# Alternating sums and weighing as a loop of 16 pairs, with all products on DVE

## The chip, the core and the metric

The kernel runs on one core of a Trainium2 chip. The metric is the time of one execution on the device in microseconds (us). A core has TensorE (PE), VectorE (DVE), ScalarE (ACT), GpSimd (POOL) and SyncE (SP), which run their own instruction streams and meet at semaphores. TensorE multiplies a stationary operand, which a weight load brings in, with a moving one, and writes to PSUM.

## What is computed

The reference is a compressed interaction network of two layers, for 512 samples with 39 fields of 64 values each, in float32:

```python
x0 = x                                  # (512, 39, 64)
h1 = einsum('bid,bjd,ijh->bhd', x0, x0, W0)   # W0 (39, 39, 128)
h2 = einsum('bid,bjd,ijh->bhd', x0, h1, W1)   # W1 (39, 128, 128)
out = concatenate([h1, h2], axis=1).sum(axis=-1)   # (512, 256)
```

Since the last sum is over d, both halves of the output are weighted sums of values that don't depend on the weights: sums over d of products of two fields (first half) or three fields (second half) of one sample.

## The kernel before

Setup. TensorE multiplies W1 with the symmetric part of W0 (L568), ACT copies the result out of PSUM (L513), DVE and GpSimd add up its entries to one weight for every product of three fields (L338, L232), TensorE turns these by transposes (L576) and ACT copies them into place (L517, 27 copies). They are 105 lists of 128 x 128 weights at c0; 10 more lists for products of two fields are loaded at c1_0.

Then the samples. Two samples are a pair: the 64 values d of each are half of the 128 partitions. 64 pairs (128 samples) are a batch, 8 pairs a unit, so there are 4 batches and 32 units. For a unit:

- SP loads x_w (windows of fields, the stationary operands of the sums; L307, two places) and x_d (fields in the order in which DVE needs them; L315, three places, DS).
- The products of two fields, 4 columns of 115 slots per pair, are written to one of two places (PRODS): DVE makes most (L422, L425, semaphore prod_ready), GpSimd five small ones (L286, L290, rest_ready), and ACT copies 10 slots of single fields (L531, singles_ready).
- TensorE sums over d (L591, `sum_four`): 12 matmuls per pair of 64 rows by 32 columns, 96 per unit, into two PSUM banks per four pairs. ACT copies the banks to s0 (L542), where a slot then has 128 columns, one for each sample of the batch.
- When a batch is summed, its 115 slots are weighed (L611, `weigh`): the slot is the stationary operand of a 128 x 128 x 128 matmul, its list the moving one, and all add up in one of two output banks. ACT copies this out (L524) and sends it to memory.

A matmul of float32 shows as two MATMUL and two LDWEIGHTS records in the trace.

TensorE's order is written out by hand. The 8 units of the first batch run as a loop of two units with 4 turns. Units 8 to 31 are unrolled: behind the sums of each unit stand 14 or 15 slots of the batch before. The last batch's 115 slots come at the end. The sums of a unit wait for all three makers of its products, and each four for the banks; products of a unit wait until the sums of the unit two before are through, since they write to the same place. SP issues in its own order, and waits for each load's place to be free.

Of the kernel before, what the change touches and what calls it, by code (L numbers as in the profile page):

```python
# [23 lines left out]
FIELDS = 39  # L24
# [77 lines left out]
def cin_kernel(nc: bass.Bass, x_w: bass.AP, x_d: bass.AP, w0: bass.AP, w1: bass.AP, c1: bass.AP, out: bass.AP):  # L102
# [12 lines left out]
    PRODS, WS, DS = 2, 2, 3  # L115
    WORDS = 56064
# [3 lines left out]
    with ctx:  # L120
# [21 lines left out]
        d_0 = take(DS * UNIT * D_WORDS)  # L142
        out_sb0 = take(2 * HID)
# [12 lines left out]
        assert w0_second0 + Y_WIDTH <= d_0 and c1_second0 + SINGLES * HID <= out_sb0  # L156

        banks = [ctx.enter_context(nc.psum_tensor(f"stage{i}", [P, BANK], F32)) for i in range(6)]
        out_ps = [ctx.enter_context(nc.psum_tensor(f"out_ps{i}", [P, BANK], F32)) for i in range(2)]
# [18 lines left out]
        rest_ready = sem("rest_ready")  # L178
        singles_ready = sem("singles_ready")
        batch_done = sem("batch_done")  # L180
        out_copied = sem("out_copied")
# [37 lines left out]
        def _(pool):  # L219
# [56 lines left out]
            for u in range(UNITS):  # L276
                pool.wait_ge(d_loaded[u % DS], 16 * (u // DS + 1))
                if u < PRODS:
                    pool.wait_ge(z_ready, 1)
                else:  # L280
                    pool.wait_ge(filled, filled_through_unit(u - PRODS))
                d, to = d_0 + u % DS * UNIT * D_WORDS, prod0 + u % PRODS * UNIT * PROD
                for column, slot, w, x in TRIANGLES:
                    n, x_at = len(block(x)), d + D_AT[x]
                    if n % 2 == 0:
                        nc.gpsimd.tensor_tensor(view(to + column * LISTED + slot + n * n // 2, (PROD, UNIT), (1, n // 2)),  # L286
                                                view(x_at, (D_WORDS, UNIT), (1, n // 2)),
                                                view(x_at + n // 2, (D_WORDS, UNIT), (1, n // 2)), ALU.mult)
                for column, slot, w, b0, b1 in LONE_LISTS:
                    done = nc.gpsimd.tensor_tensor(view(to + column * LISTED + slot, (PROD, UNIT), (1, b1 - b0)),  # L290
                                                   view(d + D_B + b0, (D_WORDS, UNIT), (1, b1 - b0)),
                                                   view(d + D_LONE, (D_WORDS, UNIT), (0, b1 - b0)), ALU.mult)
                done.then_inc(rest_ready, 1)

        @block_.sync
        def _(sp):
# [13 lines left out]
            def load_listed(u):  # L310
                if u >= DS:
                    sp.wait_ge(prod_ready, u - DS + 1)
                    sp.wait_ge(rest_ready, u - DS + 1)
# [12 lines left out]

            for u in range(WS, UNITS):
                if u + 1 < UNITS and u + 1 >= DS:
                    load_listed(u + 1)
                load_windows(u)  # L330

        @block_.vector
        def _(dve):
# [78 lines left out]
            def products(u):  # L412
# [6 lines left out]
                for column, slot, w, x in TRIANGLES:  # L419
# [3 lines left out]
                         view(x_at, D, (1, whole), (1, n)), ALU.mult)  # L423
                for column, slot, w, x, x0, x1, y, g0, g1 in RECTANGLES:
# [83 lines left out]
        def _(act):  # L508
            g = 0
            for f in range(FIELDS):  # L510
                for a, b in Y_PARTS:
                    act.wait_ge(filled, g + 1)
                    nc.scalar.copy(view(y0 + f * Y_WIDTH + a, (1, b - a)), banks[g % RING][:, 0:b - a]).then_inc(emptied, 1)  # L513
                    g += 1
            for k, n in TURNS:
                act.wait_ge(filled, g + 1)
                nc.scalar.copy(view(c0 + k * HID, (1, n * HID)), banks[g % RING][:, 0:n * HID]).then_inc(emptied, 1)  # L517
                g += 1

            def take_out(n):  # L520
                act.wait_ge(batch_done, n + 1)
                if n >= 1:
                    act.wait_ge(out_stored, 16 * n)
                nc.scalar.copy(view(out_sb0, (1, 2 * HID)), out_ps[n % 2][:, 0:2 * HID]).then_inc(out_copied, 1)  # L524
                act.wait_ge(out_copied, n + 1)
                act.dma_start(out[n * B:(n + 1) * B, :], view(out_sb0, (1, 2 * HID))).then_inc(out_stored, 16)

# [6 lines left out]

            act.wait_ge(z_ready, 1)
            for u in range(PRODS):
                singles(u)
            for q in range(FOURS):
                n, t = divmod(q * FOUR, PAIRS)
                act.wait_ge(filled, SETUP_BANKS + q + 1)  # L540
# [4 lines left out]
                u = (q + 1) * FOUR // UNIT - 1  # L545
# [3 lines left out]
                if t == PAIRS - FOUR and n >= 1:  # L549
                    take_out(n - 1)  # L550
# [4 lines left out]
        def _(pe):  # L555
# [43 lines left out]
            def weigh(n, k):  # L599

                if k == 0:
                    pe.wait_ge(emptied, emptied_through_four((n + 1) * PAIRS // FOUR - 1))
                    if n == 0:
                        pe.wait_ge(c1_ready, 1)
                    if n >= 2:
                        pe.wait_ge(out_copied, n - 1)
# [88 lines left out]
```

## Time and profile before

| | us |
|---|---|
| median of 3 runs | 345.33 (340.78 to 349.36) |
| the profiled execution | 343.26 |
| its span, first to last instruction | 341.5 |
| PE busy in it | 263.6 (77%) |
| DVE busy | 200.4 (59%) |
| ACT busy | 129.1 (38%) |
| POOL busy | 114.8 (34%) |

The profile is of one execution. Busy shares are averages over stages that differ: the setup lasts until 96.75 us, the first batch until about 140, then sums and weighing alternate until 309.65, and the last batch is weighed. "issue" stands where an engine was idle and waited for nothing that the profile shows. PE's busy time counts overlapping matmuls once.

### The profile page before, as it was taken

Reading aid. Unit: us, or ns where it says so; the run is one execution under the profiler, and the core shown is the slowest. Engines: PE = TensorE matmul, PEld = TensorE weight load, DVE = VectorE, ACT = ScalarE, POOL = GpSimd, SP = SyncE. Lnnn points to the kernel's source line nnn. Section 1 sums busy time; section 2 is a strip of 40 time slices with the busy share of each in tenths; the row PEclk is TensorE's granted clock in tenths of the full one; section 3 lists DMA queues with packets and bytes.
Section 4 is the critical chain, followed back from the end, with each engine's and each line's share of the span. In section 5 each row is a group of like instructions: output and inputs, shape, how many; then the busy total and the mean of one; then the engine's idle time right before and its main releaser. Section 6 shows DMA issues by size and latency. Waiting matters only on the chain.

```text
span 341.5 us, 16183 instructions
## 1 busy us (share of the span) xinstructions
PE 263.6 (77%) x7325; PEld 226.8 (66%) x7325; DVE 200.4 (59%) x671; ACT 129.1 (38%) x270; POOL 114.8 (34%) x284
## 2 busy tenths in 40 slices
PE   0999999206946516848988788899798878889997
PEld 0555555106935515738878778788788778779996
DVE  1125599999436977935567675686577766730000
ACT  1477777203954415511333234323343224322000
POOL 9425596304022694662233222332232222300000
PEclk9999999755996968876999999999999999999999
DMA  7800000400034625622334443353335433200000
GB/s 263 370 0 0 5 0 0 161 1 0 2 111 136 184 68 189 195 56 101 101 101 145 114 142 118 105 192 103 102 112 168 131 105 103 73 23 19 0 2 15
DMA packets 10860, 32.56 MB, mean 95 GB/s; under 512 B 1200, under 2 KB 1712, under 8 KB 10672
## 3 DMA queue, kind: packets, MB, share of 16 engines
q1 hardware_dynamic: 10224, 31.15, 28.4%
q8 instruction: 48, 0.79, 0.9%
q10 hardware_dynamic: 576, 0.52, 0.4%
q14 instruction: 12, 0.10, 0.1%
HBM read 31.14 MB, written 0.52 MB: 93 GB/s over the span
## 4 chain that ended last, share of the span: by engine, by line
PE 70%; issue 17%; DVE 5%; ACT 4%; DMA 2%; POOL 2%; SPq 0%; DVEq 0%; POOLq 0%
PE out_ps L611 31%; PE stage L591 22%; PE stage L568 16%; DVE arena L425 3%; ACT arena L517 3%; DVE arena L422 2%; DMA arena<-in_w 2%; PE stage L576 2%; POOL arena L286 1%; ACT arena L542 0%; ACT arena L531 0%; POOL arena L290 0%; SPq L298 0%; SPq L297 0%; ACT arena L524 0%
## 5 line engine op out<-in xcount | busy, mean ns | idle before, releaser
L591 PE MATMUL stage<-arena 64*32 64x115 f32 (+4 forms) x6144 | 87.0, 244 | 45.2 <-issue 32.6
L611 PE MATMUL out_ps<-arena 128*128 128x128 f32 x920 | 111.3, 280 | 4.4 <-issue 4.4
L542 ACT COPY arena<-stage 128x460 f32<-128x460 f32 x128 | 63.1, 545 | 132.9 <-PE stage L591 131.4
L611 PEld LDWEIGHTS out_ps<-arena 128*128 128x128 f32 x920 | 106.5, 194 | 9.1 <-issue 8.6
L591 PEld LDWEIGHTS stage<-arena 64*32 64x32 f32 x6144 | 75.5, 110 | 53.7 <-issue 51.0
L286 POOL TENSOR_TENSOR arena<-arena 128x24 f32<-128x24 f32 x96 | 52.8, 575 | 158.7 <-PE stage L591 144.1
L422 DVE TENSOR_TENSOR arena<-arena 128x224 f32<-128x224 f32 (+1 forms) x192 | 62.1, 389 | 71.2 <-PE stage L591 71.1
L425 DVE TENSOR_TENSOR arena<-arena 128x392 f32<-128x392 f32 (+5 forms) x288 | 91.4, 386 | 0.0
L568 PE MATMUL stage<-arena 128*128 128x390 f32 x156 | 54.3, 511 | 7.7 <-DMA arena<-in_w 7.7
L338 DVE TENSOR_TENSOR arena<-arena 128x294 f32<-128x294 f32 (+30 forms) x189 | 47.5, 327 | 15.1 <-ACT arena L513 15.0
L568 PEld LDWEIGHTS stage<-arena 128*128 128x128 f32 x156 | 30.8, 198 | 30.5 <-issue 10.4
L513 ACT COPY arena<-stage 128x390 f32<-128x390 f32 x78 | 37.7, 484 | 22.7 <-PE stage L568 22.7
L232 POOL COPY arena<-arena 128x6 f32<-128x6 f32 (+21 forms) x117 | 28.4, 303 | 24.4 <-ACT arena L513 24.4
L576 PE MATMUL stage<-arena 128*128 128x128 f32 x105 | 14.1, 306 | 18.1 <-issue 18.1
L576 PEld LDWEIGHTS stage<-arena 128*128 128x128 f32 x105 | 13.9, 161 | 18.7 <-issue 18.7
L290 POOL TENSOR_TENSOR arena<-arena 128x88 f32<-128x88 f32 x64 | 23.0, 379 | 0.0
L517 ACT COPY arena<-stage 128x512 f32<-128x512 f32 (+1 forms) x27 | 13.5, 682 | 20.0 <-PE stage L576 20.0
L531 ACT COPY arena<-arena 128x320 f32<-128x320 f32 x32 | 15.8, 505 | 0.0
L524 ACT COPY arena<-out_ps 128x256 f32<-128x256 f32 x4 | 1.5, 372 | 33.9 <-PE out_ps L611 33.9
L220 POOL MEMSET arena<- 128x13440 f32 x1 | 11.3, 11298 | 0.3 <-POOLq L684 0.3
L435 DVE TENSOR_TENSOR arena<-arena 128x1280 f32<-128x1280 f32 x1 | 1.5, 1492 | 9.9 <-DMA arena<-in_c 9.9
L432 DVE TENSOR_TENSOR arena<-arena 128x780 f32<-128x780 f32 x1 | 1.0, 971 | 5.0 <-DMA arena<-in_w 5.0
(7 smaller groups left out, 2.2 us busy)
## 6 DMA issues: line engine op xcount, KB each, us to landing
arena<-in_x_d SPq DMA_DIRECT2D x32, 448.0 KB, 4.0
arena<-in_x_w SPq DMA_DIRECT2D x32, 360.0 KB, 3.3
arena<-in_w SPq DMA_DIRECT2D x1, 1344.0 KB, 10.1
arena<-in_c SPq DMA_DIRECT2D x2, 640.0 KB, 11.7
arena<-in_w SPq DMA_DIRECT2D x2, 390.0 KB, 3.4
arena<-in_w SPq DMA_DIRECT2D x1, 768.0 KB, 7.4
out<-arena ACTq DMA_DIRECT2D x4, 128.0 KB, 1.7
arena<-in_w SPq DMA_DIRECT2D x1, 384.0 KB, 5.9
```

The source lines that it names most:

```text
L232: return nc.gpsimd.tensor_copy(view(to, *to_axes), view(at, *axes))
L286: nc.gpsimd.tensor_tensor(view(to + column * LISTED + slot + n * n // 2, (PROD, UNIT), (1, n // 2)), view(x_at, (D_WORDS, UNIT), (1, n // 2)),
L338: return nc.vector.tensor_tensor(view(to, *to_axes), view(a, *a_axes), view(b, *b_axes), ALU.add)
L422: mult(view(at, T, (n, whole), (1, n)), view(x_at, D, (0, whole), (1, n)), view(x_at, D, (1, whole), (1, n)), ALU.mult)
L425: done = mult(view(to + column * LISTED + slot, T, (g1 - g0, x1 - x0), (1, g1 - g0)), view(d + D_AT[x] + x0, D, (1, x1 - x0), (0, g1 - g0) ...
L513: nc.scalar.copy(view(y0 + f * Y_WIDTH + a, (1, b - a)), banks[g % RING][:, 0:b - a]).then_inc(emptied, 1)
L517: nc.scalar.copy(view(c0 + k * HID, (1, n * HID)), banks[g % RING][:, 0:n * HID]).then_inc(emptied, 1)
L542: nc.scalar.copy(view(s0[n % 2] + s * PAIRS + t, (B, LISTED), (1, FOUR)), banks[2 * (q % 2) + s][:, 0:LISTED * FOUR].rearrange("p (n b) -> ...
L568: nc.tensor.matmul(claim(g)[:, 0:b - a], view(w1_0 + f * HID, (1, HID)), view(w0_0 + a, (1, b - a)), start=True, stop=True).then_inc(fille ...
L576: done = nc.tensor.transpose(bank[:, m * HID:(m + 1) * HID], view(z0 + (k + m) * B, (1, B)), view(ident0, (1, HID)))
L591: done = nc.tensor.matmul(banks[2 * four_place + s][WIDE * column:WIDE * (column + 1), 0:LISTED * FOUR] .rearrange("p (n b) -> p b n", b=F ...
L611: done = nc.tensor.matmul(to, view(s0[n % 2] + k * B, (1, B)), weights, start=k == 0, stop=k == LISTED - 1, skip_group_check=True)
```

## The change

- Units 8 to 31 are no longer unrolled on TensorE but a loop over three batches with a loop of 4 turns inside, each of two units: 16 pairs. Its instructions are the same in each turn, so the slots to weigh must lie at a fixed place: ACT copies 13 slots a unit of the batch before to t_0, in a half of 6 and one of 7, and TensorE weighs them from there. The list (moving operand) is found by an address in a register. The 11 slots left (all 10 singles and one) are copied and weighed behind each batch's last unit. The last batch is weighed unrolled and from s0, as before.
- There is one output bank instead of two. A matmul with zeros (GpSimd clears the identity for that) begins it for both halves.
- DVE makes the five small products as well, 20 instructions a unit instead of 15; GpSimd makes none, and rest_ready is gone.
- x_d has two places instead of three (the room goes to t_0), and SP issues each unit's x_d just ahead of its x_w, one unit later than before.
- ACT copies the singles of the first two units ahead of the turned lists instead of behind them.

TensorE, where unit 8 ends and its first weighing stands; stage are the banks of sums, out_ps the output's. Before:

```order
L591 MATMUL stage<-arena 32x57 x2
L591 MATMUL stage<-arena 32x115 x4
L611 MATMUL out_ps<-arena 128x128 [waits c1_ready,emptied]
L611 MATMUL out_ps<-arena 128x128 x13
L591 MATMUL stage<-arena 32x49 [waits singles_ready,rest_ready,emptied,prod_ready,w_loaded1]
```

And now, in the inner loop (ISA is a fused instruction of two to four register operations):

```order
L614 MATMUL stage<-arena 32x57 x2
L614 MATMUL stage<-arena 32x115 x4
L678 ISA [waits staged]
L630 MATMUL out_ps<-arena 128x128
L630 ISA
L630 MATMUL out_ps<-arena 128x128
L630 ISA
L630 MATMUL out_ps<-arena 128x128
L630 ISA
L630 MATMUL out_ps<-arena 128x128
```

A register instruction now stands between each two slots, and a wait for ACT's copy ahead of each half.

ACT in a unit of the later batches; L542 and L557 empty the banks of sums, L531 and L509 copy the singles. Before:

```order
L542 COPY arena<-stage 128x115x4 [waits filled]
L542 COPY arena<-stage 128x115x4
L542 COPY arena<-stage 128x115x4 [waits filled]
L542 COPY arena<-stage 128x115x4
L531 COPY arena<-arena 128x32x10 [waits d_loaded0]
```

And now:

```order
L541 COPY arena<-arena 128x768 [waits weighed]
L541 COPY arena<-arena 128x896 [waits weighed]
L557 COPY arena<-stage 128x115x4 [waits filled]
L557 COPY arena<-stage 128x115x4
L557 COPY arena<-stage 128x115x4 [waits filled]
L557 COPY arena<-stage 128x115x4
L509 COPY arena<-arena 128x32x10 [waits d_loaded0]
```

Two copies of 6 and 7 slots stand ahead of the banks, and wait for TensorE's weighing of the half before in the same place.

The diff, cut to what is spoken of:

```diff
-    PRODS, WS, DS = 2, 2, 3
+    PRODS, WS, DS = 2, 2, 2
+
+    IN_BATCH = PAIRS // UNIT
+    EACH = PAIRED // IN_BATCH
+    HALVES = [(0, EACH // 2), (EACH // 2, EACH)]
+    REST = LISTED - IN_BATCH * EACH
+    REST_HALVES = [(0, EACH // 2), (EACH // 2, REST)]
...
-            for u in range(UNITS):
-                pool.wait_ge(d_loaded[u % DS], 16 * (u // DS + 1))
...
+            pool.wait_ge(filled, SETUP_BANKS)
+            nc.gpsimd.memset(ident, 0.0).then_inc(out_free, 1)
...
-            for u in range(WS, UNITS):
-                if u + 1 < UNITS and u + 1 >= DS:
-                    load_listed(u + 1)
+            for u in range(DS, UNITS):
+                load_listed(u)
                 load_windows(u)
...
+                    if n % 2 == 0:
+                        mult(view(at + n * n // 2, T, (1, n // 2)), view(x_at, D, (1, n // 2)),
+                             view(x_at + n // 2, D, (1, n // 2)), ALU.mult)
+                for column, slot, w, b0, b1 in LONE_LISTS:
+                    mult(view(to + column * LISTED + slot, T, (1, b1 - b0)), view(d + D_B + b0, D, (1, b1 - b0)),
+                         view(d + D_LONE, D, (0, b1 - b0)), ALU.mult)
...
+            def stage(first, a, b, half):
+                if half >= 2:
+                    act.wait_ge(weighed, half - 1)
+                nc.scalar.copy(view(t_0 + a * B, (1, (b - a) * B)), view(first + a * B, (1, (b - a) * B)))\
+                    .then_inc(staged, 1)
...
+                if n >= 1 and t % UNIT == 0:
+                    for i, (a, b) in enumerate(HALVES):
+                        half = (n - 1) * IN_ALL + v * len(HALVES) + i
+                        stage(s0[(n - 1) % 2] + (SINGLES + v * EACH) * B, a, b, half)
...
+            def begin_out():
+                nothing = view(ident0, (1, HID))
+                nc.tensor.matmul(out_ps[:, 0:2 * HID], nothing, view(ident0, (0, 2), (1, HID)), start=True, stop=False,
+                                 skip_group_check=True)
...
+            def weigh_staged(v, a, b):
+                for k in range(a, b):
+                    done = weigh(t_0 + k * B, c0 + k * HID + v * (EACH * HID), False)
+                done.then_inc(weighed, 1)
...
+            def turn(w_wanted, unit_wanted, banks_wanted, behind):
+                for v in range(PRODS):
+                    pe.wait_ge(w_loaded[v], w_wanted)
+                    pe.wait_ge(prod_ready, unit_wanted)
+                    pe.wait_ge(singles_ready, unit_wanted)
+                    pe.reg_add(unit_wanted, unit_wanted, 1)
+                    for half in range(2):
+                        pe.wait_ge(emptied, banks_wanted)
+                        pe.reg_add(banks_wanted, banks_wanted, 2)
+                        sum_four(v, half, half)
+                    behind(v)
+                pe.reg_add(w_wanted, w_wanted, 16)
...
+                with pe.Fori(1, BATCHES):
+                    pe.wait_ge(out_free, out_wanted)
+                    pe.reg_add(out_wanted, out_wanted, 1)
+                    begin_out()
+                    with pe.Fori(0, IN_BATCH, PRODS) as first:
+                        def weigh_unit(v):
+                            for a, b in HALVES:
+                                staged_half()
+                                weigh_staged(first + v, a, b)
+                        turn(w_wanted, unit_wanted, banks_wanted, weigh_unit)
+                    for a, b in REST_HALVES:
+                        staged_half()
+                        weigh_rest(t_0, t_0 + SINGLES * B, a, b).then_inc(weighed, 1)
```

## Rows read from the trace of the kernel before

**Rows 1.** Stages; columns: stretch, length, PE, PEld, DVE, ACT, POOL busy, clock, DMA.
```profile
96.75:139.96 43.21, 23.37 (x1536) 20.77 (x1537) 32.39 (x106) 18.13 (x39) 21.73 (x36) 0.80 0.49 146
139.96:161.68 21.72, 15.06 (x448) 13.75 (x452) 13.28 (x45) 5.36 (x12) 12.50 (x15) 0.76 0.38 117
161.68:309.65 147.97, 127.45 (x4829) 118.40 (x4829) 95.35 (x300) 50.66 (x108) 36.42 (x100) 1.00 0.36 112
```

**Rows 2.** Groups of PE, 161.68 to 309.65; columns: form, count, busy, mean ns, idle before.
```profile
L611 PE MATMUL out_ps<-arena 128*128 128x128 f32 x605 | 73.5, 279 | 3.5 <-issue 3.5
L591 PE MATMUL stage<-arena 64*32 64x115 f32 (+4 forms) x4224 | 57.2, 233 | 17.0 <-issue 17.0
```

**Rows 3.** The chain of waits, 176 to 185 us; columns: start, length, what.
```profile
175.99 2.39 PE stage L591 x116
178.38 3.32 PE out_ps L611 x28
...
183.25 0.91 issue
```

**Rows 4.** The timeline of PE, first batch and unit 9; columns: start, length, group, idle before.
```profile
106.16 1.23 PE L591 MATMUL stage<-arena 64*32 64x49 f32 x47 [2.16 <-issue]
...
107.56 2.73 PEld L591 LDWEIGHTS stage<-arena 64*32 64x32 f32 x192 [0.59 <-issue]
107.59 2.95 PE L591 MATMUL stage<-arena 64*32 64x49 f32 x192 [0.20 <-issue]
...
112.93 2.45 PE L591 MATMUL stage<-arena 64*32 64x49 f32 x192 [2.39 <-issue]
...
127.04 3.25 PE L591 MATMUL stage<-arena 64*32 64x49 f32 x192 [7.35 <-POOL arena L290]
...
149.72 2.11 PE L591 MATMUL stage<-arena 64*32 64x49 f32 x114 [2.86 <-issue]
```

**Rows 5.** The timeline of DVE and POOL in the first batch.
```profile
107.49 2.02 DVE L422 TENSOR_TENSOR arena<-arena 128x224 f32<-128x224 f32 x6 [3.40 <-PE stage L591]
...
109.44 3.20 DVE L425 TENSOR_TENSOR arena<-arena 128x392 f32<-128x392 f32 x9
...
115.53 10.51 POOL L286 TENSOR_TENSOR arena<-arena 128x24 f32<-128x24 f32 x3 [3.20 <-PE stage L591]
...
116.88 1.64 DVE L422 TENSOR_TENSOR arena<-arena 128x224 f32<-128x224 f32 x6
...
118.44 2.82 DVE L425 TENSOR_TENSOR arena<-arena 128x392 f32<-128x392 f32 x9
...
121.18 1.64 DVE L422 TENSOR_TENSOR arena<-arena 128x224 f32<-128x224 f32 x6
...
139.36 9.59 POOL L286 TENSOR_TENSOR arena<-arena 128x24 f32<-128x24 f32 x3 [4.27 <-PE stage L591]
```

**Rows 6.** DMA queues; columns: queue, kind, packets, MB, share of 16 engines.
```profile
q8 instruction: 48, 0.79, 0.9%
```

**Rows 7.** Groups of ACT, each shape apart, whole span.
```profile
L542 ACT COPY arena<-stage 128x460 f32<-128x460 f32 x128 | 63.1, 545 | 132.9 <-PE stage L591 131.4
...
L531 ACT COPY arena<-arena 128x320 f32<-128x320 f32 x32 | 15.8, 505 | 0.0
```

**Rows 8.** The timeline where the setup ends.
```profile
93.51 2.44 ACT L517 COPY arena<-stage 128x512 f32<-128x512 f32 x5
...
95.57 1.10 ACT L531 COPY arena<-arena 128x320 f32<-128x320 f32 x2
...
96.75 2.95 PE L591 MATMUL stage<-arena 64*32 64x49 f32 x210 [2.55 <-ACT arena L531]
```

**Rows 9.** The loads of x_d: from issue to landing.
```profile
DMA to landing us min/median/max: 3.3/4.0/4.9
```

**Rows 10.** The end of the chain of waits; columns as in rows 3.
```profile
309.72 29.24 PE out_ps L611 x260
...
338.98 0.37 ACT arena L524
```

More of the change, by code:

```diff
@@ L142, in cin_kernel @@
         d_0 = take(DS * UNIT * D_WORDS)
+        t_0 = take(EACH * B)
         out_sb0 = take(2 * HID)
@@ L155, in cin_kernel @@
         c1_second0 = d_0 + Y_WIDTH
-        assert w0_second0 + Y_WIDTH <= d_0 and c1_second0 + SINGLES * HID <= out_sb0
+        assert REST <= EACH and w0_second0 + Y_WIDTH <= d_0 and c1_second0 + SINGLES * HID <= out_sb0
         banks = [ctx.enter_context(nc.psum_tensor(f"stage{i}", [P, BANK], F32)) for i in range(6)]
-        out_ps = [ctx.enter_context(nc.psum_tensor(f"out_ps{i}", [P, BANK], F32)) for i in range(2)]
+        out_ps = ctx.enter_context(nc.psum_tensor("out_ps", [P, BANK], F32))
         RING = len(banks)
@@ L508, in _, with singles @@
         def _(act):
+            def singles(u):
+                act.wait_ge(d_loaded[u % DS], 16 * (u // DS + 1))
+                nc.scalar.copy(view(prod0 + u % PRODS * UNIT * PROD, (PROD, UNIT), (LISTED, 4), (1, SINGLES)),
+                               view(d_0 + u % DS * UNIT * D_WORDS + D_SINGLES, (D_WORDS, UNIT), (SINGLES, 4), (1, SINGLES)))\
+                    .then_inc(singles_ready, 1)
             g = 0
@@ L514, in _ @@
                     g += 1
+            act.wait_ge(z_ready, 1)
+            for u in range(PRODS):
+                singles(u)
             for k, n in TURNS:
@@ L549, in _ @@
                 if t == PAIRS - FOUR and n >= 1:
+                    (a, b), (_, c) = REST_HALVES
+                    half, s_at = n * IN_ALL - len(REST_HALVES), s0[(n - 1) % 2]
+                    stage(s_at, a, b, half)
+                    act.wait_ge(weighed, half)
+                    nc.scalar.copy(view(t_0 + b * B, (1, (SINGLES - b) * B)), view(s_at + b * B, (1, (SINGLES - b) * B)))
+                    nc.scalar.copy(view(t_0 + SINGLES * B, (1, (c - SINGLES) * B)),
+                                   view(s_at + (SINGLES + IN_BATCH * EACH) * B, (1, (c - SINGLES) * B)))\
+                        .then_inc(staged, 1)
                     take_out(n - 1)
@@ new lines, in weigh_staged, with weigh_rest @@
+            def weigh_staged(v, a, b):
+                for k in range(a, b):
+                    done = weigh(t_0 + k * B, c0 + k * HID + v * (EACH * HID), False)
+                done.then_inc(weighed, 1)
+            def weigh_rest(s_at, last_at, a, b):
+                for k in range(a, b):
+                    if k < SINGLES:
+                        done = weigh(s_at + k * B, c1_0 + k * HID, True)
+                    else:
+                        done = weigh(last_at, c0 + (PAIRED - 1) * HID, False, stop=True)
+                return done
@@ L647, in _, with staged_half @@
-            for k in range(LISTED):
-                weigh(BATCHES - 1, k)
+                    turn(w_wanted, unit_wanted, banks_wanted, lambda v: None)
+                pe.wait_ge(c1_ready, 1)
+                def staged_half():
+                    pe.wait_ge(staged, staged_wanted)
+                    pe.reg_add(staged_wanted, staged_wanted, 1)
+                with pe.Fori(1, BATCHES):
[11 more added lines that the diff above has]
+                        weigh_rest(t_0, t_0 + SINGLES * B, a, b).then_inc(weighed, 1)
@@ L651 @@
+            s_at = s0[(BATCHES - 1) % 2]
+            pe.wait_ge(out_free, BATCHES)
+            begin_out()
+            pe.wait_ge(emptied, emptied_through_four(FOURS - 1))
+            for k in range(IN_BATCH * EACH):
+                weigh(s_at + (SINGLES + k) * B, c0 + k * HID, False)
+            weigh_rest(s_at, s_at + (LISTED - 1) * B, 0, REST).then_inc(weighed, 1)
 def kernel(r_x, L0_rec_W0, L0_rec_W1):
```

92 lines of the change are left out of this document (19 added, 73 removed).

## The prediction

> **What bounds the kernel now.** The profiled execution took 343.26 us, its span is 341.5; the 1.8 between them is kept. It lies 2.1 under the median of the runs, 345.33. I read the busy time by stage first, then the groups of the longest stage, then the chain of waits, then the timeline where they left a question.
>
> By stage [rows 1]: the reader is to see that TensorE is busy 127.45 of 147.97 us in the long stretch, but only 23.37 of 43.21 in the first batch and 15.06 of 21.72 behind it, and that no other engine comes near it in the long stretch (DVE 95.35). In that stretch the two kinds of matmul stand side by side [rows 2]: 4224 records are 22 units of 192, 605 are 302 slots at two records each, and TensorE is idle for 20.5 us with nothing named as the releaser ("issue").
>
> One unit without and one with such a gap [rows 3]: the sums of a unit last 2.39 us, 14 slots of weighing 3.32, so 0.237 a slot, and in the next unit 0.91 us of nothing lie inside the sums. What the gaps are the first batch tells [rows 4]. There the code is a loop of two units. In its first turn TensorE stops in the middle of sums for 2.16 us at 106.16; in later turns 192 records run through in one piece (2.45 us at 112.93), on the same engine with the same kind of work. And the instruction queue fetched 48 packets, 0.79 MB, 16.4 KB each [rows 6]. 7325 matmul records and as many weight loads were executed; less three repeats of 768 that is 12,346, or 257 a packet: each instruction was fetched once, the loop's too. So the gaps are fetches of new code, which a second turn of a loop does not need.
>
> DVE and GpSimd set the first batch [rows 5]. DVE makes the products of a unit in 4.30 us (116.88 to 121.18) when it works alone. A GpSimd multiplication that starts at 115.53 does not end until DVE pauses; TensorE waits 7.35 us for it, until 127.04 [rows 4]. It happens again at 139.36, and the sums of unit 9 start only at 149.72 [rows 4, 5].
>
> **The change, part by part.**
>
> *Start of unit 0.* The two copies of singles stood behind ACT's last copy of the turned lists (end 95.95); unit 0 started at 96.75, just behind them [rows 8]. They now stand ahead of the 27 copies, where ACT waited for the first transposes anyway. Unit 0 starts at 96.03: -0.7.
>
> *DVE takes the five small products.* 6 multiplications of 1104 elements take 1.56 us and 9 of 2040 take 2.74 [rows 5], start to start: 68 ns each plus 1.04 ns an element. Five more with 216 elements: 0.57 us, 4.87 us a unit. In the long stretch that hides: DVE starts when a unit's sums end and must be done one weighing, one set of sums and one weighing later (3.1 + 2.4 + 3.1 us). In the first batch it is the bound. The first turn is as before, with its fetches: the sums of unit 1 ended 0.20 before 107.59 [rows 4] and now end 0.7 earlier, at 106.7; products 3 end at 111.6, then one unit each 4.87: products 8 end at 136.0 and the sums of unit 8 begin at **136.1**. Before they began at 139.96, and the next unit lost ten more.
>
> *Two places instead of three for the lists.* A load is issued when the products two units earlier are made and has 4.87 us; the loads take 3.3 to 4.9, median 4.0 [rows 9]. I cost it at nothing; at its slowest, with signals and issue 0.4 more, it adds 0.4 a unit in five units, 2 us. SP also asks for the lists one unit later than before, still behind the same product.
>
> *Code of units 8 to 31 as a loop of 12 turns.* Goes: 20.5 us of gaps in 22 units [rows 2] and those of units 8 and 9. Comes: a first pass through some 900 new instructions, 3 us by the 0.9 to 2.2 us of such gaps [rows 3, 4]. Comes too: at each unit register arithmetic, waits and every second time a branch. In the first loop that cost TensorE 0.20 us, its weight loads 0.59 [rows 4]; I take **0.4** at each unit.
>
> *Weighing by register address.* 13 slots a unit instead of 14.4, and 11 behind each batch. Each slot now has a fused register instruction ahead of it and a moving operand whose address a register holds. No row shows that form. From below: it hides under the 0.237 us that the array needs for a slot (nothing). A gain is excluded, since the same two passes stream. From above: 0.59 us for the six steps at a turn is 0.1 a step; with the dispatcher's share in the 0.4 us before that perhaps 0.15. Three slow steps a slot (register instruction, two passes) make 0.30 to 0.45, that is 0.06 to 0.21 too much for 312 slots, 20 to 66 us. I take nothing, since steady dispatch should be nearer to the middle of a stream than to a turn's branch and four waits, and keep both ends.
> The Trainium skill ("TensorE: Matmul & The Clock Gate", Wait — 56ns, not 53.3ns?) gives about 62 ns for a matmul that its sequencer decodes in software. By that the two passes would take 0.12 us, under 0.237, and my sum would stand; no run here shows the figure.
>
> *ACT copies 13 slots a unit, in halves.* 768 and 896 elements; from 320 elements in 0.505 us [rows 7] at best 0.88 and 0.99 (at 0.85 ns an element, the slope from 256 elements in 0.37 us [rows 10] to 460 in 0.545), at worst, by proportion, 1.21 and 1.41. With four copies of 0.545 and one of 0.505, overlapping a little, ACT has 4.4 to 5.3 us in a unit of 5.9. A half is copied as soon as TensorE is through with its predecessor, one unit ahead of need, so it hides; if it did not, ACT's lateness would be added to each unit.
>
> *One output bank, cleared by a matmul.* At each of three later batches TensorE waits for the copy-out (0.37 us as in [rows 10], with signals 0.6) and clears 256 columns (0.4): 3 us in all. GpSimd has nothing left, hence no stuck multiplication.
>
> **The sum.** 136.1; 24 units of 2.39 + 13 x 0.237 = 5.47: 131.3; 33 slots behind batches: 7.8; 24 x 0.4: 9.6; outputs 3; first pass 3. That is 290.8. The last 115 slots at 0.225 (29.24 us for 130 [rows 10]): 25.9; from there to the end of the span 2.5. Span 319.2, time **321.0**: 22 under the profiled execution, 7% under the median. Two per cent, 7 us here, is about what a measurement of this kernel tells from no change.
>
> **The rivals.**
>
> *The dispatcher becomes the bound, mildly (0.20).* A slot takes 0.25 to 0.32 us and the 0.4 becomes 0.6: 321 + 4 to 26 + 5, or 330 to 352. For it: three slow steps against 0.237 leaves little. The profile would show equal gaps between weighing matmuls.
>
> *The same, strongly (0.11): slower than before.* The place is the weighing in units 8 to 31, the price (slot - 0.237) x 312, and it decides from 0.337 us a slot: 321 + 31 = 352, 2% over the median. At 0.45 the time is 387. For it: the turn's six steps already take 0.1 each; against: mid-unit register steps leave no mark in 2.45 us of sums.
>
> *Code is fetched again at each turn (0.06): slower.* A turn would fetch 3.6 blocks. Before, 4829 x 2 instructions were 37.7 blocks for 20.5 us: 0.54 each; 12 turns add 23. The branch back would wait for its block, 2.16 seen plus the 1.6 us that the block ahead lasts: 43 more. 321 + 23 + 43 - 3 = 384. Against: [rows 6], and the turn at 107.59 that cost 0.20. For: the body is 909 instructions, the first loop's 780.
> The Trainium skill ("Runtime: NRT & Kernel Launch", Instruction fetch mechanics) has this rule: a taken branch out of a two-page window forces a fetch. By that rule it is 384; the trace of the first loop speaks against it.
>
> *Everything turns but the feeders are late (0.08).* DVE keeps its slower pace, 2.02 + 3.20 us [rows 5] plus 0.57, in the first batch (+6), or loads add 2, or ACT adds 2 at a batch's start: 325 to 334.
>
> *More comes back (0.05).* Boundaries hide wholly and the first pass under DVE: 308 to 313. That leaves **0.50** for the forecast, 313 to 330.
>
> **Numbers.** Faster by over 2% (under 338.4): 0.50 + 0.08 + 0.05 and half of the mild rival, 0.72. Within 2%: its other half and a bit, 0.11. Slower: 0.17. The range takes in the forecast, late feeders and most of the mild rival: 312 to 345.
>
> **What will show it.** PE's instruction queue with some 11 packets instead of 48. Products of a unit in 4.87 us; unit 8 near 136. Weighing at 0.237 a slot in units 8 to 31, against 0.225 in the tail, shows the register address right or wrong; gaps at each second unit show the branch. Weight-load gaps inside sums in later turns would prove me wrong on fetching, ACT's L541 as a releaser on staging.

## The result, and where the time went

| | us | ratio to before, 95% interval |
|---|---|---|
| before, median of 4 runs | 346.7 (340.78 to 349.36) | |
| changed kernel, median of 4 runs | 310.63 (309.65 to 311.24) | 0.905 (0.894 to 0.916) |
| predicted | 321.0, range 312 to 345 | 0.93 |

It is 9.5% faster. The ratio is taken over the runs in the faster of two states that executions of these kernels show (of before, 340.78 and 345.33), so it is not the quotient of the medians. The cause forecast is the one that the trace shows, and the gain is larger than forecast: 310.63 lies 10.4 under the predicted time and 1.4 under the range. The profiled execution took 310.69 us, its span is 308.9, so 1.8 lie outside the span as before.

The span is 32.6 shorter. Read at four marks that both traces have:

| | before | after | difference |
|---|---|---|---|
| up to the sums of unit 0 | 96.75 | 95.25 | -1.5 |
| units 0 to 7, up to the sums of unit 8 | 43.21 | 39.44 | -3.8 |
| units 8 to 31, up to the last batch's weighing | 169.76 | 146.00 | -23.8 |
| weighing of the last batch, and the end | 31.8 | 28.2 | -3.6 |

Marks of before are in [rows 1, 8, 10]; those of after follow. First the stages of the changed kernel, with the columns of [rows 1]:

```profile
95.25:134.69 39.44, 24.46 (x1538) 21.44 (x1539) 34.58 (x142) 19.70 (x41) 0.00 (x0) 0.83 0.53 157
134.69:279.99 145.30, 140.83 (x5302) 132.55 (x5302) 113.81 (x460) 103.24 (x178) 0.00 (x0) 1.00 0.40 128
```

In the first batch DVE is busy 34.58 of 39.44: it is still the bound there, behind the fetches of the loop's first turn. In the long stretch TensorE is busy 140.83 of 145.30, so 4.5 us are left of what were 20.5 in 22 units [rows 2]. ACT has come from 50.66 us of the long stretch of before to 103.24 here, and still TensorE waits for it only at the end of a batch, for the copy-out (0.38 in the chain below). From the page, the instruction queue and the two groups of matmuls (columns as in [rows 2]):

```profile
q8 instruction: 10, 0.16, 0.2%
...
L630 PE MATMUL out_ps<-arena 128*128 (+1 forms) x920 | 109.5, 278 | 1.3 <-issue 1.3
...
L614 PE MATMUL stage<-arena 64*32 64x115 f32 (+4 forms) x6144 | 82.9, 243 | 19.2 <-issue 11.6
```

Ten packets instead of 48 [rows 6]: at 256 instructions each that is 2560, while the 7333 matmul records and as many weight loads that were executed are 57 times 256. So the loops were not fetched again at each turn. Slots with a register address ahead of them have the mean of before (278 ns against 279).

The chain of waits from the first pass of the new loop on:

```profile
134.69 2.44 PE stage L614 x109
137.14 1.09 PE out_ps L630 x8
138.23 1.34 issue
139.57 2.27 PE out_ps L630 x18
141.84 1.30 PE stage L614 x67
143.15 1.57 issue
144.72 1.28 PE stage L614 x47
146.00 3.10 PE out_ps L630 x26
149.09 2.38 PE stage L614 x117
...
176.51 2.38 PE stage L614 x115
178.90 5.57 PE out_ps L630 x48
...
184.49 0.38 ACT arena L532
184.87 0.12 issue
185.00 0.67 PE out_ps L625 x2
...
280.69 25.70 PE out_ps L630 x230
...
```

Three things are to be seen. The first pass has two holes, 1.34 and 1.57, and the pieces of work beside them last 0.5 longer than in later units (14.41 us up to 149.10 for two units that later take 2 x 5.48). From 146.00 on a unit is 3.10 + 2.38 = 5.48 us with nothing between them, neither at a unit nor, every second time, at the branch. And a batch costs a copy of 0.38, 0.12 and a clear of 0.67 between 5.57 of weighing (24 slots) and the next sums. Apart from the first pass and these three pauses, the long stretch is TensorE's own work, end to end. The outer loop, which spans the inner one and the slots behind it, comes back without a gap too.

In units 10 to 31, 147.97 us before [rows 1] and 131.66 now (149.03 to 280.69), the gaps took 20.5. The bare work of before was 22 x 2.39 + 302 x 0.237 = 124.2, its busy time 127.45. The other 3.3 lie in sums that a gap cuts in two: they last 2.54 to 2.75 us in the chain of before instead of 2.39, here 1.55 + 1.01:

```profile
181.70 1.55 PE stage L591 x76
183.25 0.91 issue
184.16 1.01 PE stage L591 x45
```

The granted clock of that stretch was 1.00 [rows 1], so it is not the clock that draws them out. What does, no run here shows.

### The profile page after: what moved, and what is told of

It is laid out like the page before. It is cut to its first block, busy times and chain, and to the rows that moved or that the text cites. A ratio compares the mean times of both kernels' runs of the same rounds, so it can differ in the third digit from the quotient of the medians.

```text
span 308.9 us, 16634 instructions
## 1 busy us (share of the span) xinstructions
PE 259.3 (84%) x7333; PEld 224.4 (73%) x7333; DVE 208.3 (67%) x831; ACT 176.7 (57%) x327; POOL 40.6 (13%) x125
## 4 chain that ended last, share of the span: by engine, by line
PE 77%; issue 10%; DVE 6%; ACT 5%; DMA 2%; SPq 0%; DVEq 0%
PE out_ps L630 35%; PE stage L614 22%; PE stage L591 17%; ACT arena L524 4%; DVE arena L422 3%; DVE arena L413 2%; DMA arena<-in_w 2%; PE stage L599 1%; PE out_ps L625 1%; ACT arena L557 1%; ACT arena L532 0%; DVE arena L419 0%; DVE arena L416 0%; SPq L292 0%; SPq L291 0%
## 5 line engine op out<-in xcount | busy, mean ns | idle before, releaser
L630 PE MATMUL out_ps<-arena 128*128 (+1 forms) x920 | 109.5, 278 | 1.3 <-issue 1.3
L630 PEld LDWEIGHTS out_ps<-arena 128*128 128x128 f32 x920 | 104.8, 192 | 5.8 <-issue 5.8
L614 PE MATMUL stage<-arena 64*32 64x115 f32 (+4 forms) x6144 | 82.9, 243 | 19.2 <-issue 11.6
L614 PEld LDWEIGHTS stage<-arena 64*32 64x32 f32 x6144 | 74.2, 110 | 25.5 <-issue 23.0
L422 DVE TENSOR_TENSOR arena<-arena 128x392 f32<-128x392 f32 (+5 forms) x288 | 90.4, 386 | 0.0
L557 ACT COPY arena<-stage 128x460 f32<-128x460 f32 x128 | 63.2, 545 | 31.4 <-PE stage L614 28.8
L413 DVE TENSOR_TENSOR arena<-arena 128x224 f32<-128x224 f32 (+1 forms) x192 | 58.2, 344 | 31.2 <-PE stage L614 31.2
L541 ACT COPY arena<-arena 128x768 f32<-128x768 f32 (+1 forms) x51 | 44.8, 883 | 22.8 <-PE out_ps L630 21.8
L509 ACT COPY arena<-arena 128x320 f32<-128x320 f32 x32 | 15.5, 488 | 18.9 <-DVE arena L329 17.5
L416 DVE TENSOR_TENSOR arena<-arena 128x24 f32<-128x24 f32 x96 | 17.0, 177 | 0.0
L419 DVE TENSOR_TENSOR arena<-arena 128x88 f32<-128x88 f32 x64 | 11.9, 227 | 0.0
```

Of the source, the lines that this page charges most:

```text
L413: mult(view(at, T, (n, whole), (1, n)), view(x_at, D, (0, whole), (1, n)), view(x_at, D, (1, whole), (1, n)), ALU.mult)
L422: done = mult(view(to + column * LISTED + slot, T, (g1 - g0, x1 - x0), (1, g1 - g0)), view(d + D_AT[x] + x0, D, (1, x1 - x0), (0, g1 - g0) ...
L541: nc.scalar.copy(view(t_0 + a * B, (1, (b - a) * B)), view(first + a * B, (1, (b - a) * B)))\
L557: nc.scalar.copy(view(s0[n % 2] + s * PAIRS + t, (B, LISTED), (1, FOUR)), banks[2 * (q % 2) + s][:, 0:LISTED * FOUR].rearrange("p (n b) -> ...
L614: done = nc.tensor.matmul(banks[2 * four_place + s][WIDE * column:WIDE * (column + 1), 0:LISTED * FOUR] .rearrange("p (n b) -> p b n", b=F ...
L630: return nc.tensor.matmul(out_ps[:, 0:HID] if single else out_ps[:, HID:2 * HID], view(s_at, (1, B)), view(c_at, (1, HID)), start=False, s ...
```

## The experiments

Each ratio is to runs of the kernel before on the same chip. Differences in us are to the 310.63 of the changed kernel, which was not run again beside them; three variants that turned out equal to it, on two chips, took 309.26 to 310.76. The first two experiments take the change apart in two steps.

**All products on DVE, and nothing else.** Edit on the kernel before:

```diff
-            for u in range(UNITS):
-                pool.wait_ge(d_loaded[u % DS], 16 * (u // DS + 1))
...
+                    if n % 2 == 0:
+                        mult(view(at + n * n // 2, T, (1, n // 2)), view(x_at, D, (1, n // 2)),
...
-                pe.wait_ge(rest_ready, u + 1)
```

> The kernel before, with the five small products made by DVE instead of GpSimd; TensorE's code stays unrolled. Theory (two separate gains: no new code to fetch, no stuck GpSimd): only the second gain shows. DVE's unit is 4.87 us, unit 8 starts 3 to 5 us earlier, unit 9 some 6 to 9 us earlier, the gaps inside sums stay, about 1.3 us a unit; 8 us less than before, ratio 0.97 to 0.98, and the instruction queue still has 48 packets. Rival (most of the 36 us came from GpSimd and DVE getting in each other's way all along): 320 us or less, ratio under 0.93.

Measured: 336.02 us, ratio 0.970 (0.958 to 0.982), 48 instruction packets. The profiled execution, 339.92, is the longest of the four, so only what DVE sets is read from it:

```profile
135.04 3.37 PE L578 MATMUL stage<-arena 64*32 64x49 f32 x192 [1.52 <-DVE arena L412]
```

The sums of unit 8 start at 135.04 and those of unit 9 at 141.90, 4.9 and 7.8 earlier than before (139.96 and 149.72), as expected. This part is worth some 11 us.

**The changed kernel with units 8 to 31 written out.** Staging, one output bank and fixed lists remain, the loop goes:

```diff
-                with pe.Fori(1, BATCHES):
+                for n in range(1, BATCHES):
...
-                    with pe.Fori(0, IN_BATCH, PRODS) as first:
+                    for v in range(IN_BATCH):
+                        u = n * IN_BATCH + v
```

> The changed kernel with the loop over units 8 to 31 written out, so that the same matmuls stand there with fixed addresses; everything else as changed. Theory (the gaps are fetches of new code): some 47 packets on TensorE's instruction queue instead of 10, gaps inside sums of 0.5 to 2 us a unit, 310.6 + 20 to 26 = 331 to 337 us. Rival (the loop itself gives nothing, the gain came from the staging, the single output bank or GpSimd): 309 to 313 us.

Measured: 341.47 us, ratio 0.988 (0.975 to 1.000). From the page and the timeline of TensorE (start, length, group, idle time before it):

```profile
q8 instruction: 48, 0.79, 0.9%
...
L614 PE MATMUL stage<-arena 64*32 64x115 f32 (+4 forms) x6144 | 86.6, 243 | 39.8 <-issue 34.0
```

```profile
154.11 0.75 PE L614 MATMUL stage<-arena 64*32 64x66 f32 x40 [2.46 <-issue]
154.79 3.17 PE L630 MATMUL out_ps<-arena 128*128 128x128 f32 x26
157.89 2.42 PE L614 MATMUL stage<-arena 64*32 64x49 f32 x189
162.18 0.38 PE L614 MATMUL stage<-arena 64*32 64x115 f32 x3 [1.86 <-issue]
162.49 4.80 PE L630 MATMUL out_ps<-arena 128*128 128x128 f32 x26
```

The 48 packets are back, and so are the gaps in the sums, 2.46 and 1.86 here. So the loop by itself is worth 341.47 - 310.63 = 30.8 us by the medians, 340.68 - 310.69 = 30.0 by the two executions whose traces are read: nearly three times what the products on DVE bring. What comes with it costs 341.47 - 336.02 = 5.4, known to a few us only, since the runs of the two kernels spread by 6.4 and 5.5. 3.5 of it are the three pauses for copy-out and clear. Staging, the order of loads and the order of ACT's copies were not taken apart further. That the three differences add up to the whole is no check, since each is taken from the one before. The loop gives more than its gaps: idle before the sums falls by 20.6 against the changed kernel, and 7.5 more lie in busy time. Half of that are the sums (86.6 against 82.9 in the loop), cut in two as above. The other half is the weighing (113.3 against 109.5), and where it lies is seen in the second row of 26 records: 4.80 us instead of 3.17 for the same 13 slots. By stretch, with the columns of [rows 1]:

```profile
162.50:167.20 4.70, 4.70 (x27) 4.59 (x26) 4.53 (x20) 2.20 (x4) 0.00 (x0) 0.64 0.56 180
167.30:172.60 5.30, 5.30 (x218) 5.11 (x218) 3.15 (x14) 4.13 (x7) 0.00 (x0) 1.00 0.37 106
```

Behind these two gaps the granted clock is 0.64 on average, so much of that stretch at the lower of its two levels, and 1.00 right after. A gap can so be paid for twice, though not each one is: most rows of 13 slots take 3.17 here too, and in the long stretch of before the clock was 1.00 with gaps of up to 1.89. I had expected the loop at 20 to 26 us, from the gaps alone.

**Small products back on GpSimd in the changed kernel.** The edit is the reverse of the first, with the wait for rest_ready in the loop.

> The changed kernel with the five small products back on GpSimd. Theory: a GpSimd multiplication gets stuck where DVE works without a pause, in the first batch, once or twice, 4 to 6 us each; behind it DVE needs 4.3 to 5.2 us of TensorE's 5.48 a unit, so that little more is lost: 315 to 322 us. Rival (GpSimd is harmless in a loop of TensorE): 307 to 311 us, since DVE's unit is shorter in the first batch.

Measured: 319.56 us, ratio 0.920 (0.905 to 0.935), 8.9 more than the changed kernel and as expected. GpSimd in the first batch, the end of DVE's products there, and TensorE:

```profile
104.88 1.14 POOL L297 TENSOR_TENSOR arena<-arena 128x24 f32<-128x24 f32 x3 [5.44 <-PE stage L629]
...
109.06 9.65 POOL L297 TENSOR_TENSOR arena<-arena 128x24 f32<-128x24 f32 x3 [2.35 <-DMA arena<-in_x_d]
...
127.64 9.61 POOL L297 TENSOR_TENSOR arena<-arena 128x24 f32<-128x24 f32 x3 [2.39 <-DMA arena<-in_x_d]
```

```profile
115.41 2.82 DVE L437 TENSOR_TENSOR arena<-arena 128x392 f32<-128x392 f32 x9
```

```profile
119.70 6.11 PE L629 MATMUL stage<-arena 64*32 64x49 f32 x384 [7.32 <-POOL arena L301]
...
138.25 3.34 PE L629 MATMUL stage<-arena 64*32 64x49 f32 x192 [7.35 <-POOL arena L301]
```

A group of three multiplications takes 1.14 us in one unit and 9.6 in two others, and TensorE waits 7.3 us both times, as in [rows 4, 5]. (A third one, at 145.92, takes 5.34.) DVE works from 104.84 to 118.23 without a pause, and the group that starts at 109.06 ends only behind that. Yet a busy DVE is not the whole condition: the group at 104.88 started together with DVE's products and took 1.14, and in the trace of before one that started in the midst of them, at 110.69, took 1.02. The stuck multiplication follows the placement on GpSimd, not the unrolled code or the third place for x_d.

**The list by a fixed address.** One line; the slots are then weighed with the first unit's lists:

```diff
-                                weigh_staged(first + v, a, b)
+                                weigh_staged(v, a, b)
```

> The changed kernel where the weighing of staged slots always takes the lists of the first two units: fixed addresses, no register instruction for them, the same number and shape of matmuls (the second half of the output is weighed with the wrong lists for that). Theory (the register address hides under the array's 0.238 us a slot): 310.6 within 0.5 us. Rival (it costs a little at each slot or each half): 2 to 10 us less.

Measured: 310.45 us, ratio 0.898 (0.890 to 0.906); the changed kernel 310.63. Register address and register instruction cost nothing that can be measured, as expected. How near that is to costing something, three doses tell.

**More register arithmetic ahead of each slot.** One register is counted up and down behind every slot; the number is 4, 12 or 48:

```diff
                     done = weigh(t_0 + k * B, c0 + k * HID + v * (EACH * HID), False)
+                    for i in range(12):
+                        pe.reg_add(spent, spent, 1 if i % 2 == 0 else -1)
```

As built these come to 5 operations in one instruction a slot, 9 in two and 27 in three, where the changed kernel has 3 in one.

> The changed kernel with more register arithmetic ahead of each staged slot: nine operations in two register instructions instead of three in one. Theory (the dispatcher runs ahead of the array and has time to spare in the 0.238 us of a slot): 310.6 within 1 us, slots still 0.238. Rival (one instruction with three operations already fills the slot): two instructions add 0.05 to 0.1 us a slot, 312 slots, 326 to 342 us.

> The same with 27 operations in three register instructions ahead of each staged slot. Both theories agree that there is a dose at which the dispatcher is the bound; its price then is what a slot takes. If an operation costs 5 to 10 ns and an instruction 30 to 60, the dispatcher needs 0.25 to 0.45 us a slot and the kernel takes 315 to 380 us. If the slots still take 0.238 us, the register work was never near the bound.

> The changed kernel with five register operations instead of three ahead of each staged slot, still in one instruction. From the two larger doses (nine operations in two instructions: 0.345 us a slot; 27 in three: 0.71) an operation costs some 0.02 us, so that three operations leave the dispatcher at 0.2 of the array's 0.238. Theory (the change sits just under the bound): five operations make 0.24, the slots stay within 0.01 of 0.238 and the kernel takes 310 to 314 us. Rival (the cost is one of instructions, not of operations; one instruction is far from the bound): no change at all, 309.5 to 311.

The middle and the large dose are one run each (348.99 and 490.88 us, both above all that was expected), the small one four (311.75 us, ratio 0.898, 0.891 to 0.905). The weighing of 13 slots, from the timelines of 4 and of 12, and one slot (two records) of 48:

```profile
159.65 3.17 PE L630 MATMUL out_ps<-arena 128*128 x26
```

```profile
153.60 2.45 PE L614 MATMUL stage<-arena 64*32 64x49 f32 x192 [0.46 <-issue]
155.98 4.41 PE L630 MATMUL out_ps<-arena 128*128 x26
```

```profile
181.28 0.48 PE L630 MATMUL out_ps<-arena 128*128 x2 [0.23 <-issue]
```

A slot takes 0.238 us with 3 and with 5 operations, 0.339 with 9 and 0.71 (0.48 and 0.23) with 27. From 9 to 27 an operation costs 0.021, if the third instruction costs nothing of its own. But by that price alone five operations would need 0.339 - 4 x 0.021 = 0.256 a slot, and 13 slots 3.3 us. They took 3.17. So an instruction has a price too, some 0.02 us at least, an operation less than 0.02, and the three operations in one instruction of the changed kernel need at most 0.20 a slot (an estimate from these three doses). It is under the array's 0.238 by a sixth or more. The rival of a bounding dispatcher was not far off, but two operations more did not bring it about. In the middle dose a gap of 0.46 stands at every second unit: once the dispatcher has no lead, the turn shows.

**Longer bodies.** Four units a turn, and a whole batch of eight:

```diff
-                    with pe.Fori(0, IN_BATCH, PRODS) as first:
+                    with pe.Fori(0, IN_BATCH, 4) as first:
```

> The changed kernel with four units in a turn of the inner loop, two turns a batch, 1816 instructions instead of 909. Theory (instructions stay near TensorE once fetched, up to a size that before's loop of 780 and the new one of 909 have not reached): 13 or 14 packets, a first pass with 3 us more of gaps, 313 to 315 us. By the Trainium skill (Runtime: NRT & Kernel Launch, Instruction fetch mechanics), which gives TensorE room for 2048 instructions, it still fits. Rival (there is room for little more than 1000): each turn is fetched again, 30 or more packets, 325 to 340 us.

> The changed kernel with all eight units of a batch in one turn, three turns in all, 3593 instructions a turn, with fixed addresses. Theory (fetched code stays only while there is room, and the room is under 3593): all three turns are fetched, some 46 packets, gaps as in the unrolled kernel, 335 to 345 us. Rival (a loop is free whatever its size): 18 packets, gaps only in the first turn, 318 to 324 us.

Measured: 371.08 us, ratio 1.080 (1.069 to 1.091), for four units, whose inner body is 1816 instructions; 355.25, ratio 1.032 (1.021 to 1.043), for eight, 3593. Both are slower than any time expected for them, the first by 31 us. The instruction queue brought 59 packets in the one and 53 in the other. The row of the first, then its TensorE where it branches back:

```profile
q8 instruction: 59, 0.97, 1.0%
```

```profile
158.90 0.59 PE L614 MATMUL stage<-arena 64*32 64x115 f32 x30 [1.64 <-issue]
...
165.88 1.03 PE L614 MATMUL stage<-arena 64*32 64x49 f32 x75 [3.29 <-issue]
168.59 2.37 PE L614 MATMUL stage<-arena 64*32 64x49 f32 x117 [1.68 <-issue]
170.89 4.79 PE L630 MATMUL out_ps<-arena 128*128 x26
```

All blocks are fetched at every turn. The changed kernel's 10 packets less the 3.6 of its body leave 6.4 for the rest of the program. So six turns of the body of 1816, 7.1 blocks of 256, took some 52.6 packets, 8.8 a turn, and three turns of the body of 3593, 14.0 blocks, took 46.6, 15.5 a turn. That is the body, its edges and perhaps a block ahead. The branch back waits 3.29 and, a block later, 1.68, and the weighing behind them is at the low clock again (4.79). 49 more packets cost 60.5 us, 1.2 each; in the body of eight units 43 more cost 44.6, 1.0 each; the straight code's 38 more cost 30.8, 0.8 each.
The Trainium skill ("Runtime: NRT & Kernel Launch", Instruction fetch mechanics) gives TensorE room for 2048 instructions, and says too that a taken branch out of a two-page window forces a fetch. The second does not hold here: bodies of 909 and, in the large dose, 964 instructions stayed (10 and 11 packets), though they are three and a half blocks. The first would let 1816 stay, and they did not; but with 8.8 packets a turn the body took more than eight blocks of 256, so that these runs do not show the room to be smaller than 2048. The largest body that stayed is 964, the smallest that did not is 1816; no run narrows it.

**Registers set ahead of the wait.** TensorE sets five registers behind its wait for the last list copy. Moved ahead of it:

```diff
-            pe.wait_ge(emptied, SETUP_BANKS)
...
+                pe.wait_ge(emptied, SETUP_BANKS)
                 with pe.Fori(0, IN_BATCH // PRODS):
```

> The changed kernel with the registers of the loops set before TensorE waits for the last turned list instead of after. Theory (the 0.86 us between ACT's last copy of a list, 94.38, and the first sums, 95.25, are this housekeeping, that the two copies of singles hid before): the gap shrinks to 0.2 to 0.4 us, 0.4 to 0.6 us less. Rival (the gap is the branch into the loop and its waits, which stay behind the wait for the list): no change.

Measured: 309.26 us, ratio 0.894 (0.889 to 0.900). The sums now begin at 93.85:

```profile
91.45 1.98 ACT L524 COPY arena<-stage 128x512 f32<-128x512 f32 x4
...
93.85 2.95 PE L614 MATMUL stage<-arena 64*32 64x49 f32 x210 [2.23 <-ACT arena L524]
```

The copies end at 93.43, so 0.42 lie between them and the sums instead of 0.87: that half microsecond is shown in the trace. That the whole kernel is faster is not: the medians differ by 1.4 us and the intervals of the ratios overlap.

**Lists between the first units.** The other idle time of the setup: ten list groups stay ahead of units 0 and 1, the rest goes behind the first batch, where TensorE waits for DVE anyway.

```diff
+            TURNS_AT = {0: TURNS[:5], 1: TURNS[5:10], 2: TURNS[10:]}
...
-                with pe.Fori(0, IN_BATCH // PRODS):
+                turn(w_wanted, unit_wanted, banks_wanted, lambda v: None, turn_lists)
+                with pe.Fori(0, IN_BATCH // PRODS - 1):
```

> A version that should beat both kernels. The first batch is a chain of DVE's products, 4.87 us a unit, that stands still from 88 until 98 us, because the sums of unit 0 wait for all 27 turned lists. Here TensorE turns 5 lists of four, sums unit 0, turns 5 more, sums unit 1, does the other three turns of the loop, and turns the last 17 behind the first batch; one more bank of PSUM serves the lists. Theory (DVE's chain is the bound of the first batch): products 2 start near 87 us instead of 97.8, unit 7's sums end near 120 instead of 132, then 8 us of lists, unit 8 at 127 to 129 instead of 134.7: 303 to 306 us. Rival (a first pass through another 780 instructions, and a TensorE that has no idle time left to hide it): 308 to 312 us.

Measured: 310.76 us, ratio 0.896 (0.891 to 0.902), 13 instruction packets: no change, as the rival had it. Units 0 and 1 are now written out ahead of the loop, so the code of two units is fetched twice, and where time was won it is lost again:

```profile
87.75 0.55 PE L623 MATMUL stage<-arena 64*32 64x49 f32 x23 [3.01 <-issue]
...
100.63 2.15 PE L623 MATMUL stage<-arena 64*32 64x49 f32 x126 [2.63 <-issue]
104.42 5.41 PE L623 MATMUL stage<-arena 64*32 64x58 f32 x306 [1.64 <-issue]
...
127.29 6.69 PE L609 MATMUL stage<-arena 128*128 128x128 f32 x53 [0.37 <-ACT arena L529]
...
135.68 2.46 PE L623 MATMUL stage<-arena 64*32 64x49 f32 x192
```

Three packets more go with gaps of 9.2 us in the first units (0.76, 3.01, 1.14, 2.63 and 1.64), where the changed kernel has 3.8 (1.17 and 2.65). The sums of unit 7 end at 125.4 instead of the expected 120, the 8 us of lists follow, and unit 8 begins at 135.68 instead of 134.69.

## Why the prediction was right, and where it was not

**What bounds the kernel.** Right. The gaps were fetches of code that is executed once: taking the loop away brings the 48 packets and 30.8 us back.

**The sum, term by term**, in us:

| term | predicted | measured |
|---|---|---|
| start of unit 0 | 96.0 | 95.25 |
| DVE, a unit of the first batch | 4.87 | 4.87 |
| sums of unit 8 begin | 136.1 | 134.69 |
| 24 units of sums and 13 slots | 24 x 5.47 | 24 x 5.48 |
| 33 slots behind batches | 7.8 | 3 x (5.57 - 3.10) = 7.4 |
| **24 unit boundaries** | **9.6** | **0** |
| outputs | 3 | 3 x 1.17 = 3.5 |
| first pass | 3 | 14.41 - 2 x 5.48 = 3.45 |
| last 115 slots | 25.9 | 25.70 |
| end | 2.5 | 2.5 |
| span | 319.2 | 308.9 |

**The step that failed** is the sentence "I take **0.4** at each unit". It was carried over from one gap in the first loop, 0.20 and 0.59 at 107.59 [rows 4]. That row stands just behind a fetch gap of 2.16, where the dispatcher has no lead. In steady turns the chain shows nothing of waits, register steps and branch; that they fall into a lead that the dispatcher has gained is my reading of it. The dose of 12 shows when such a cost appears: 0.46 at a turn, once each slot takes the dispatcher longer than the array. The 9.6 us are nearly the whole miss of 10.3 in the span. The forecast's mechanism stood; this term of it was sized from a row of another state. The case "more comes back", 308 to 313, had the time and half of the reason: the boundaries hide wholly, the first pass does not. With 0.05 I gave it too little: it was no separate event but the other end of a cost that I had only bounded. The other differences are small or chance. The sums of unit 8 began 1.4 earlier than forecast, 0.75 of it from the start of unit 0 and 0.9 from shorter gaps in the loop's first turn (9.73 us up to the end of unit 1's sums, 10.64 before). And the first pass differs from one execution to the next: 3.45 here, 5.9 in that of the small dose, where its first gap is 2.90.

**Start of unit 0.** The -0.7 hardly came. Measured from the end of the setup's sums of weights (80.07 before, 78.74 now) unit 0 starts 16.68 and 16.51 later, so 0.17 was gained. The two copies had hidden 0.87 us of register setting that stood behind the same wait; with them gone it showed, and moving it took half of it away. The 1.33 by which the setup itself ended earlier is the executions' difference, not the change's: the first load took 5.08 us instead of 5.93, and the same 156 matmul records behind it 53.77 instead of 54.26.

**DVE takes the five small products.** Right to the hundredth:

```profile
109.95 1.21 DVE L413 TENSOR_TENSOR arena<-arena 128x224 f32<-128x224 f32 x4
...
114.83 1.21 DVE L413 TENSOR_TENSOR arena<-arena 128x224 f32<-128x224 f32 x4
...
119.70 1.21 DVE L413 TENSOR_TENSOR arena<-arena 128x224 f32<-128x224 f32 x4
```

One unit each 4.87 us, without a gap: two places for x_d were enough (median to landing 3.8), which the +2 of late loads had doubted. The margin is thin: in the trace with registers set early a load of 4.75 us holds DVE once, and one unit takes 5.12. In the long stretch DVE hid, as said.

**Weighing by register address.** Taking nothing was right, and the fixed address and the doses show why: at most 0.20 a slot against 0.238. Of my bound from above, 0.1 a step and 0.30 to 0.45 a slot, the price per step was some five times too high; like the boundary's it was read just behind a gap.

**ACT's halves.** I estimated 0.88 and 0.99 at best, and they take 0.83 and 0.94:

```profile
L541 ACT COPY arena<-arena 128x896 f32<-128x896 f32 x24 | 22.6, 941 | 15.4 <-PE out_ps L630 15.4
L541 ACT COPY arena<-arena 128x768 f32<-128x768 f32 x27 | 22.5, 832 | 7.4 <-PE out_ps L630 6.4 <-ACT arena L532 1.0
```

ACT waits for TensorE here, not the other way. They are in nobody's way.

**Code fetched again at each turn.** Wrong for this body, and right for one of twice its length. The wait at the branch was near what I had put, 3.29 and 1.68 against 2.16 and 1.6, but the whole was dearer: 60.5 us are 10.1 a turn, where the rival's prices give 7.1 x 0.54 + 3.76 = 7.6. Its 0.54 a block counts the gaps alone, not the work they draw out nor the clock behind them. A slip in its sum: 2.16 + 1.6 is 41 us for eleven branches back or 45 for twelve turns, not 43.

**The range and the chances.** The chance of faster adds up to 0.73, not 0.72. The range kept both ends of the slot's price, but only one value for the boundary. With nothing there the same sum gives 321.0 - 9.6 = 311.4, and the range had to begin below that, at the 308 of "more comes back".

**What stays open.** How long a body may be between 964 and 1816 instructions; how exactly the register cost splits between operations and instructions; what staging by itself costs; and when and why GpSimd's multiplications get stuck beside DVE, which the runs show to happen but not why.

## What to carry to other kernels

Where TensorE issues many small matmuls, count the packets of its instruction queue: about as many as the executed instructions make blocks of 256 (48 of 57 before, 10 of 57 now) mean that nearly all code is new, and a loop whose body stays resident, 909 instructions here, takes the gaps away, even if an engine with time to spare must copy operands to a fixed place for it. Before a body is made longer, or a turn peeled off ahead of it, price its fetches: here they cost 0.8 to 1.2 us a block. A fixed cost of dispatch read just behind a stall is an upper bound: here it hid as long as the instructions issued faster than the array worked, so it goes into the range from nought.

## What the hardware showed that was not expected

- A branch back in a resident loop costs nothing that shows (5.48 us a unit, with and without it), and 3.29 + 1.68 us when its code has to be fetched.
- Behind two fetch gaps, 2.46 and 1.86 us, the granted clock was 0.64 in the mean, and 13 slots took 4.80 us instead of 3.17.
- A register operation ahead of a matmul costs TensorE's dispatcher about 0.02 us where it is the bound (9 to 27 a slot); three or five in one instruction cost none of the array's time.
- Three multiplications of 128 x 24 on GpSimd took 1.14 us in one unit and 9.6 in two others, where they ended only behind DVE's products; what decides between the two is open.
